# Two attentions with heads of 8: when the output of the first batch, the layer norm statistics and the store are made

## The reference

```
for l in 0..3:
    xn = layernorm(x)
    x  = x + attention_l(xn) * silu(ffn_l(xn))
```

```
Q, K, V = split(xn @ W (+ b))
w   = softmax(mask(Q K^T / sqrt(8)))
out = concat_heads(w V) @ Wo (+ bo)
```

## Time and profile before

| | us |
|---|---|
| median of 3 runs | 1969.68 |
| lowest and highest | 1960.73, 1974.17 |
| the profiled execution | 1975.89 |
| its span in the trace | 1973.2 |
| PE busy, DVE busy, ACT busy, POOL busy | 1748.1, 1442.3, 1152.1, 1038.0 |

### The profile page before, as it was taken

How to read it: one execution, slowest core, us unless ns; L and a number is a source line. 1 busy time by engine, 2 the same in 40 slices (tenths; PEclk the granted TensorE clock), 3 DMA queues, 4 the chain that set the end, 5 groups by cost and what they waited for, 6 DMA issues and landing times. The chain is left out here.

```text
span 1973.2 us, 34447 instructions
## 1 busy us (share of the span) xinstructions
PE 1748.1 (89%) x13171; PEld 1432.4 (73%) x13199; DVE 1442.3 (73%) x2911; ACT 1152.1 (58%) x2340; POOL 1038.0 (53%) x998
## 2 busy tenths in 40 slices
PE   6999999999999999899699699964798558999997
PEld 4888888888888888787567577753577445666675
DVE  6888888888888888534587677857777488777772
ACT  4677766666666667455367565542333344666665
POOL 4888999999999998920312134425257530110111
PEclk9999999999999999999899899966799878999999
DMA  3000000001000000000000000002045300000000
GB/s 89 14 1 14 1 14 1 14 1 36 1 1 1 1 1 1 28 1 1 20 17 17 0 2 1 2 22 70 22 107 134 77 14 1 1 1 1 2 2 23
DMA packets 52068, 37.44 MB, mean 19 GB/s; under 512 B 7528, under 2 KB 45832, under 8 KB 51904
## 3 DMA queue, kind: packets, MB, share of 16 engines
q1 hardware_dynamic: 45216, 30.53, 5.3%
q0 software_dynamic: 5632, 4.20, 1.5%
q10 hardware_dynamic: 1056, 0.52, 0.1%
HBM read 29.99 MB, written 5.24 MB: 18 GB/s over the span
## 5 line engine op out<-in xcount | busy, mean ns | idle before, releaser
L753 POOL TENSOR_TENSOR dtl<-dts,dth 128x512 fp32r<-128x512 f32 x256 | 346.8, 1355 | 20.5
L683 DVE TENSOR_REDUCE nm<-PS 128x1 f32<-128x1024 f32 x256 | 311.1, 1216 | 18.5 <-PE PS L203 17.7
L1884 ACT ACTIVATE ET_a<-PS 128x256 f32<-128x256 f32 (+2 forms) x512 | 221.7, 496 | 124.8 <-PE PS L1783 76.5
L751 POOL CAST dth<-dts 128x512 fp32r<-128x512 f32 x256 | 239.7, 936 | 56.2 <-ACT dts L610 55.1
L201 PE MATMUL PS<-xh,yh 128*128 128x512 f32 x512 | 225.4, 440 | 11.3 <-ACT G L603 5.7
L144 PE MATMUL PS<-C,XN 128*128 128x128 f32 x1120 | 177.6, 284 | 38.6 <-DVE XN L196 37.0
L203 PE MATMUL PS<-xh,yl 128*128 128x512 f32 x512 | 204.4, 399 | 0.0
L202 PE MATMUL PS<-xl,yh 128*128 128x512 f32 x512 | 204.2, 399 | 0.0
L603 ACT ACTIVATE XNT<-PS,nm 128x1024 f32<-128x1024 f32 x128 | 142.8, 1116 | 92.7 <-DVE nm L683 92.5
L1703 POOL TENSOR_SCALAR_AFFINE_SELECT ET_a<-ET_a 128x1024 f32<-128x1024 f32 x32 | 34.9, 1092 | 305.9 <-ACT ET_a L1884 305.9
L610 ACT ACTIVATE dts<-PS 128x512 f32<-128x512 f32 x256 | 152.8, 599 | 51.0 <-POOL dtl L753 50.9
(11 more groups left out here) (419 smaller groups left out, 4711.6 us busy)
## 6 DMA issues: line engine op xcount, KB each, us to landing
e_wg<-in_WgT SPq DMA_DIRECT2D x16, 256.0 KB
e_wu<-in_WuT SPq DMA_DIRECT2D x16, 256.0 KB
e_wd<-in_WdT SPq DMA_DIRECT2D x16, 256.0 KB
X<-in_L_attn_X SPq DMA_DIRECT2D x2, 512.0 KB, 4.5
wqn<-in_L_attn_Wq SPq DMA_DIRECT2D x8, 128.0 KB, 2.2
wkn<-in_L_attn_Wk SPq DMA_DIRECT2D x8, 128.0 KB, 2.5
wvn<-in_L_attn_Wv SPq DMA_DIRECT2D x8, 128.0 KB, 2.6
won<-in_WoT SPq DMA_DIRECT2D x8, 128.0 KB, 2.6
```

The costliest lines, as they stand in the source:

```text
L683: e.tensor_reduce(self.nm[:, half, i:i + 1], self.S[half], AX.X, MAX, negate=True).then_inc(*self.top.up((g, half)))
L751: e.tensor_copy(hi, src).then_inc(*ts.up((g, g4, "h")))
L753: e.tensor_tensor(lo, src, f(hi), SUB).then_inc(*ts.up((g, g4, "l")))
L1884: e.activation(dst, src, ACT.Exp, scale=self.SC, bias=0.0).then_inc(*self.ex.up(it))
```

## The change

1. The output of chunks 0 and 1 (whose heads are all in `XN` after head 15) is made within the drain. `fin` turns four tiles of `XN` into bank 7 and ScalarE copies them to a tile of `hm`; `finp` multiplies by `Wo` into bank 4 or 5; `sum` is VectorE's part, called `finish(c)`. Kind 3: fin and finp at (33, 1), (33, 4), (35, 1), (35, 4); sums at (34, 4), (36, 4). Kind 1: at (33, 1), (33, 7), (34, 1), (34, 7); sums at (37, 8), (37, 9).
2. Since banks 4 and 5 now hold those products, the columns of x >= 32 go round four banks instead of six.
3. In kind 1, give 29 moves from x = 39 to (36, 7), give 31 to (38, 1).
4. After the steps, PE turns chunks 2 and 3 one behind the other, then multiplies both.
5. `Gate1`: bn_stats two per step (x = 4 to 11), moments at x = 12, the 16 scalings at x = 14 to 29; GpSimd's power for it before cut_off(8) instead of (16); silus at place 13 of x = 36 and 37.
6. The bn_stats of `X` for layers 1 and 2 are taken chunk by chunk behind each chunk's sum (four each, in `Ffn0.add` and in `finish`), and `Prep` begins with the moments there. Layer 3 keeps its 16.
7. The store becomes three DMAs, of 512, 256 and 256 KB, behind the sums of chunks 1, 2 and 3.

```
@@ Ffn0.dve, add(c) @@
             e.tensor_tensor(x, x, st, ADD).then_inc(*self.on_dve.up(("add", c)))
+            q.wait_ge(self.on_dve, ("add", c))
+            for i in range(4 * c, 4 * c + 4):
+                t = e.bn_stats(k.st[:, i, :], k.X[:, i, :])
+            if c == 3:
+                t.then_inc(*self.stats.up("st"))
@@ Prep.dve @@
-        k.stats(e, k.X, self.ln, self.tag)
-        k.moments(e, q, self.ln, self.tag)
+        if not self.seen:
+            k.stats(e, k.X, self.ln, self.tag)
+        k.moments(e, q, self.ln, self.tag, self.seen)
@@ Gate1 @@
-        self.steps = [("st", i) for i in range(NT)] + [("r", 0)] + [("n", i) for i in range(NT)] + [("silu", i) for i in range(2)]
+        self.steps = [("st", i) for i in range(0, NT, 2)] + [("r", 0), ("none", 0)] + [("n", i) for i in range(NT)]
...
+    def silu(self, e, q, i):
+        gs = self.k.G[:, 8 * i:8 * i + 8, :]
+        q.wait_ge(self.ln, (8 * i + 7, 2))
+        e.activation(gs, gs, ACT.Silu, scale=1.0, bias=0.0).then_inc(*self.gated.up(i))
@@ Small.__init__ @@
+        self.fin_src = [f(x) for x in self.hm] + self.AVS
+        self.fin_bank = (4, 5, 2, 3)
...
-                elif hh == 3 and x >= 11:
+                elif hh == 3 and 11 <= x < 39:
                     self.misc[x, 1], self.misc[x, 7] = ("give", x - 10), ("give", x - 8)
+                elif x in (33, 34):
+                    self.misc[x, 1], self.misc[x, 7] = ("fin", x - 33), ("finp", x - 33)
+                elif x == 36:
+                    self.misc[x, 7] = ("give", 29)
+                elif x == 37:
+                    self.misc[x, 8], self.misc[x, 9] = ("sum", 0), ("sum", 1)
+                elif x == 38:
+                    self.misc[x, 1] = ("give", 31)
                 continue
...
+            if x in (33, 35):
+                m += [("fin", (x - 33) // 2), ("finp", (x - 33) // 2)]
+            elif x in (34, 36):
+                m += [("sum", (x - 34) // 2)]
...
             elif x == NH:
-                cs, cn = list(range(6)), 0
+                cs, cn = list(range(4)), 0
@@ Small.pe @@
+        def finish_turn(c, o, sig, event):
+            for j, n in enumerate(self.turned_of(c)):
+                t = k.tr(e, o[:, 128 * j:128 * j + 128], k.XN[:, n, :])
+            t.then_inc(*sig.up(event))
+
+        def finish_product(c):
+            o, src = self.k.bank(self.fin_bank[c]), self.fin_src[c]
+            q.wait_ge(self.fin_a, c)
+            q.wait_ge(w.in_wo, "w")
+            self.bank_done(q, self.fin_bank[c])
+            for j in range(4):
+                t = e.matmul(o[:, 128 * j:128 * j + 128], src[:, 128 * j:128 * j + 128], w.WO[:, :], start=True, stop=True)
+            t.then_inc(*self.fin_p.up(c))
...
-        for c in range(4):
-            if c >= 2:
-                q.wait_ge(self.fin_a, c - 2)
-            for j in range(4):
-                t = k.tr(e, k.bank(2 * c % 4)[:, 128 * j:128 * j + 128], k.XN[:, where[4 * c + j], :])
-            t.then_inc(*self.fin_t.up(c))
-            q.wait_ge(self.fin_a, c)
...
+        for c in (2, 3):
+            self.bank_done(q, c - 2)
+            finish_turn(c, k.bank(c - 2), self.fin_t, c)
+        for c in (2, 3):
+            finish_product(c)
@@ Small.act @@
+            elif (x, j) in self.misc and self.misc[x, j][0] == "fin":
+                u = self.misc[x, j]
+                for v in self.first_and_side[-2:]:
+                    self.hm_free(q, v)
+                q.wait_ge(self.mi_pe, u)
+                e.activation(self.fin_src[u[1]], k.bank(7), ACT.Copy).then_inc(*self.fin_a.up(u[1]))
+            if self.gate and j == 13 and x in (36, 37):
+                self.gate.silu(e, q, x - 36)
@@ Small.dve, finish(c) @@
+            q.wait_ge(self.gate.gated, c // 2)
+            e.tensor_tensor(o, sv, G, MUL).then_inc(*self.fin_d.up((c, 0)))
+            q.wait_ge(self.fin_d, (c, 0))
+            e.tensor_tensor(X, X, o, ADD).then_inc(*self.fin_d.up((c, 1)))
+            q.wait_ge(self.fin_d, (c, 1))
+            for i in range(4 * c, 4 * c + 4):
+                t = e.bn_stats(k.st[:, i, :], k.X[:, i, :])
@@ Finish.sp @@
-        e.dma_start(k.out.rearrange("b (n p) d -> p (b n) d", p=128), k.X[:, :, :]).then_inc(*self.stored.up("x"))
-        q.wait_ge(self.stored, "x")
+        for i, (c, t0, n) in enumerate(((1, 0, 8), (2, 8, 4), (3, 12, 4))):
+            q.wait_ge(s.fin_d, (c, s.fin_d.last[1]))
+            e.dma_start(k.out[t0 // 8].rearrange("(n p) d -> p n d", p=128)[:, t0 % 8:t0 % 8 + n, :],
+                        k.X[:, t0:t0 + n, :]).then_inc(*self.stored.up(i))
+        q.wait_ge(self.stored, 2)
```

More of the change, by code:

```diff
@@ L1152, with __init__ @@
 class Prep:
-    def __init__(self, k, where, tag, split):
-        self.k, self.tag, self.split = k, tag, split
+    def __init__(self, k, where, tag, split, seen=None):
+        self.k, self.tag, self.split, self.seen = k, tag, split, seen
         if split:
             self.xh, self.xl = k.sb(where, f"xh{tag}", [128, T], F32R), k.sb(where, f"xl{tag}", [128, T], F32R)
-        self.ln = k.sig("p_ln", k.norm_events(tag) + [(tag, "r")] + [("n", i) for i in range(NT)])
+        self.ln = k.sig("p_ln", k.norm_events(tag)[1 if seen else 0:] + [(tag, "r")] + [("n", i) for i in range(NT)])
         self.sq = k.sig("p_root", [tag])
@@ L1565, in __init__ @@
         first = [("project", 0, w_, ck) for w_, ck in ((1, 0), (0, 0), (1, 1), (0, 1))]
-        use = first + list(self.misc.values()) + [("give", x) for x in range(1, NH, 2) if ("give", x) not in self.misc.values()]
+        use = first + [u for u in self.misc.values() if u[0] not in ("finp", "sum")]
         self.first = first
+        assert all(("give", x) in use for x in range(1, NH, 2))
         self.prev_mi = {b: a for a, b in zip(use[4:], use[5:])}
@@ L1601, in of @@
                 mi.append(u)
-            else:
+            elif u[0] == "give":
                 mi.extend([u + (h,) for h in ("r", 0, 1)])
@@ L1626, in __init__, with side_free, bank_done, turned_of @@
         self.fin_d = k.sig("a_fin_sum", [(c, n) for c in range(4) for n in range(3 if kind == 3 else 2)])
+        self.fin_st = k.sig("a_fin_stats", ["st"])
+        self.seen = (self.fin_st, "st")
         self.ends = [(self.fin_p, 3), (self.fin_a, 3), (self.fin_d, self.fin_d.last), (self.cut, self.cut.last)]
         self.bq, self.bm = w.bq, w.bm
-    def done_of(self, u):
-        return u + (1,) if u[0] == "give" else u
+    def side_free(self, q, u):
+        a = self.prev_mi.get(u)
+        if a and a[0] == "fin":
+            q.wait_ge(self.fin_a, a[1])
+        elif a:
+            q.wait_ge(self.mi, a + (1,) if a[0] == "give" else a)
+    def bank_done(self, q, b):
+        a = self.bank_last[b]
+        q.wait_ge(self.top if a[0] == "row" else self.ex, a)
+    def turned_of(self, c):
+        where = {8 * b + self.tile_of(half, g): 8 * b + 4 * half + g for b in range(2) for half in range(2) for g in range(4)}
+        return [where[4 * c + j] for j in range(4)]
     @staticmethod
@@ L1819, in pe @@
                 side(self.misc[x, j])
-        for u in self.use:
-            if u[0] == "give" and u not in self.misc.values():
-                side(u)
-        where = {8 * b + self.tile_of(half, g): 8 * b + 4 * half + g for b in range(2) for half in range(2) for g in range(4)}
         q.wait_ge(self.mi, self.mi.last)
-        for b in range(6):
-            a = self.bank_last[b]
-            q.wait_ge(self.top if a[0] == "row" else self.ex, a)
-        for c in range(4):
-            if c >= 2:
-                q.wait_ge(self.fin_a, c - 2)
-            for j in range(4):
-                t = k.tr(e, k.bank(2 * c % 4)[:, 128 * j:128 * j + 128], k.XN[:, where[4 * c + j], :])
-            t.then_inc(*self.fin_t.up(c))
-            q.wait_ge(self.fin_a, c)
-            q.wait_ge(w.in_wo, "w")
-            if c >= 2:
-                q.wait_ge(self.fin_d, (c - 2, 0))
-            for j in range(4):
-                t = e.matmul(k.bank((2 * c + 1) % 4)[:, 128 * j:128 * j + 128], self.AVS[c % 2][:, 128 * j:128 * j + 128], w.WO[:, :],
-                             start=True, stop=True)
-            t.then_inc(*self.fin_p.up(c))
+        for c in (2, 3):
[3 more added lines that the diff above has]
+            finish_product(c)
     def act(self, e, q):
@@ L1894, in act @@
             project(u, k.bank(n))
-        late = 0
         for x, j in self.steps():
@@ L1902, in act @@
                 project(self.misc[x, j], k.bank(7))
-            if self.gate and j == 3 and x >= 4 and late < len(self.gate.steps):
-                self.gate.act_step(e, q, late)
-                late += 1
+            elif (x, j) in self.misc and self.misc[x, j][0] == "fin":
[6 more added lines that the diff above has]
+                self.gate.silu(e, q, x - 36)
             if x == 0 and j == 13:
                 clear(1, 1)
-        for c in range(4):
+        for c in (2, 3):
             q.wait_ge(self.fin_t, c)
-            if c < 2:
```

(13 more changed lines are left out.)

91 lines of the change are left out of this document (44 added, 47 removed).

## The result

Over 20 runs of each, the changed kernel takes 1961.04 us (median; 1956.76 to 1965.16) and the kernel before 1971.57 (1960.73 to 1976.12). The ratio is 0.9947 with a 95% interval of 0.9935 to 0.9960: 10.4 us less, between 7.9 and 12.8. The profiled execution took 1959.83, its span is 1957.4.

A forecast was written before the change was run, and what follows sets the result against it. No single engine bounds the kernel: PE is busy longest, layers have different limits, and the change touches only seams and drains. Gains 1.4 + 8.2 + 2.2 = 11.8 off the median 1969.68 give 1957.9, range 1949 to 1967.

The forecast's parts named there:

- Start of layer 1: Border of layers 0 and 1: eight of 16 bn_stats leave the path, 1.6 less 0.2 for waits, 1.4 gained.
- Steady part of layer 1: VectorE's Gate1 step ahead of the maxima sets group length: 1.9 lost, and 0.8 earlier possible at x = 32.
- Drain of layer 1: Layer 1, steps 33 and 34 on: turn, copy and product make the drain end 1.1 later, bounds 0 and 2.8.
- End of layer 1: Moments of layer 2 start 11.2 sooner relative to old times; first-batch sums cost nothing but fill the whole slack.
- End of layer 3: Chunks 0 and 1 are gone from the end; last sum at 1963.5 instead of 1968.12, 4.6 saved.
- Store: End of layer 3: last store 256 KB, 2.25 less waiting; rival reading of the large-transfer rule cancels it, 1960.2.
- Drain of layer 3: Steps 33 to 36: four banks and new work cost 1.85 + 0.5 + 1.85 + 0.5 = 4.7, bounds 1.0 and 7.
- A: Rival: layer 3's drain absorbs the new work and four banks, paying only 1.0; 1954.2, chance 0.18.
- B: Rival: PE's clock stays at the upper level at layer 1's end, worth about 3; 1954.9, chance 0.14.
- C: Rival, slower: PE's clock falls in layer 3's drain, costing 16; 1973.9, chance 0.04.
- D: Rival: layer 1's late sums overrun, steady part loses double, drains reach upper bounds, 2 + 2 + 4 less; 1966, chance 0.09.
- one of the forecast's signs of being wrong: Anywhere in the profile: a stretch the change does not touch moves by more than 2.

The follow-up runs named there:

- experiment 9: Kernel before with only layer 0's border bn_stats taken chunk by chunk; moments 4.67 behind the gate of chunk 2, router's reduce 18.07 behind the moments.
- experiment 6: Changed kernel with the Gate1 step of every fourth head behind both sums of the maxima; median 1955.07 us, ratio 0.9927.
- experiment 7: Changed kernel with layer 1's sum 1 behind give 31; moments of layer 2 come 14.12 behind the last mask, 1.89 earlier.
- experiment 10: Changed kernel with one 1 MB store in place of three; span ends 4.96 behind the issue, 2.35 later than with three pieces.
- experiment 1: Kernel before with four banks instead of six in layer 3's drain; steps 33 to 36 take 24.41, 2.98 more than before.
- 2: Changed kernel with both first-batch products of layer 3 in bank 5 and five banks for columns; steps 33 to 36 take 25.13, 0.76 less.
- 5: Changed kernel with layer 3's first-batch products in bank 7 and six banks for columns; steps 33 to 36 take 24.79, 1.1 less.
- experiment 3: Changed kernel with the copy of bank 7 on VectorE instead of ScalarE, both layers; odd steps 6.63 and 6.53, even ones 6.15 and 6.14.
- experiment 4: As experiment 3, with layer 3's first-batch product at place 6 instead of 4; odd steps 6.68 and 6.69, steps 33 to 36 together 25.64.
- experiment 8: On top of experiment 7, filler turns of the identity on PE; moments of layer 2 13.29 behind the last mask, layer 1's router's reduce 4.8 later.

## Why the prediction was right

The forecast was 1957.9, a ratio of 0.9940 to the median it was taken from; measured are 0.9947 and 1961.04. The base itself moved: 1969.68 over three runs, 1971.57 over twenty, which is 1.9 of the 3.1 between. The rest, 1.2, is inside the interval. The mechanism holds seam by seam, with one term, the start of layer 1, whose gain no run shows, and one, the end of layer 1, that met its number to 0.2 where the same code varies by 1.1.

- **Start of layer 1**, 1.4 gained: 1.37 to the moments, but not at the router, to which the way goes with PE's clock (experiment 9). The step said "leave the path" and stopped at the moments. From the gate of chunk 2 to the router's reduce the new code took 22.5 to 22.9 in every trace without fillers there, the old 22.4 and 27.0, so what the change is worth at the router stays open. Without this term the forecast's sum is 10.4.
- **Steady part of layer 1**, 1.9 lost and 0.8 back: the four terms that can be read match to 0.02. That the step's place is what counts is shown by experiment 6.
- **Drain of layer 1**, 1.9 from x = 32 to the last mask, measured 2.15.
- **End of layer 1**, 11.2: 11.03, and 10.0 against the 25.98 of experiment 9. "The first-batch sums cost nothing" holds against the kernel before: PE's turn of chunk 2 starts 7.56 behind the last mask in both traces. "They fill the whole slack" was too small a word. The forecast's own times had give 31 waiting 1.0 on VectorE (turn ready 1304.3, sums done 1305.3); measured are 1.97, because the clock stayed up until about 1301.2, behind the sums of head 31, and the turn was ready 4.90 behind the last mask and not 5.76. (In the trace of before the clock had fallen at 1300.1.) So 1.9 were left lying there (experiment 7).
- **End of layer 3**, 4.6: 4.90. **Store**, 2.25: 2.35, and the same by experiment 10. The rate of the old transfer, times the bytes no longer behind the last sum, was the right price, and the rival reading by the Trainium skill's rule falls.
- **Drain of layer 3**, 4.7: 4.46, and by the forecast's own measure, the loads, its parts hold too: 1.85 for an odd step was 1.68, 0.5 for an even one 0.57. The walk through step 33 had the copy done 2.2 into it, the product loaded at 3.2 and column 7 at 3.6; in the trace it is 2.17, 3.20 and 3.35. That the even steps pay less for the banks holds as well (0.64 against 0.87, experiment 1). What the experiments add: in the odd steps the number of banks makes no difference once turn and product are there (2 and 5), in the even ones all of the 0.57 is banks (5).

Of the rivals, A (the drain pays only 1.0) falls with experiment 1: the banks alone are 3.0. B (clock stays up at the end of layer 1) did not happen, and where fillers made it happen, on top of experiment 7, it was worth 0.8 and not 3. C did not happen: the drain of layer 3 ran at 1.00 with PE busy for 24.62 of 25.90. D did not either: the late sums kept the old times, and neither the steady part nor the drains reached D's bounds. By its letter one of the forecast's signs of being wrong came true, that a stretch without a change moves by more than 2: layer 0's attention moved by 5.3. The sign was set too tight, since before and experiment 1 have the same code up to layer 3 and differ there by 3.2, and by 6.0 at the gate.

How the odd steps' 1.7 divides between PE's new loads (0.59 and 0.97) and its wait for the copy (0.79) is not shown: experiment 3 left 0.61 of the wait, and experiment 4 put two waits for banks in its place. A late product with six banks would tell, and was not run. The fall of the clock at different times behind the same code is described and not explained. The 5.4 of layer 0 and the 0.8 between router and x = 4 stay open.

## What to carry to other kernels

Work that is moved into a drain whose engines have no room costs time there (here 1.7 per step that held turn and product, at both places tried), and the buffers it takes are a second price (here 0.6 per step between), which can be had back if it uses the buffer it has just emptied. Two ways of cutting a pipeline into steps give the same sum and different parts, so compare a forecast's parts with the measure they were forecast in. In a queue, put what others wait for ahead of what only has to be done: the order of two sums was worth 1.9, the place of a normalization step ahead of or behind the sum of the maxima 3.4. Add up the seams by distances between events of one trace, since the total of a profile carries the drift of every stage before.

## What the runs showed of the hardware

VectorE's operations with both inputs in SBUF that were begun while GpSimd's affine_select ran lasted up to 1.1 in place of 0.29 and ended 0.15 behind it (experiment 6; one begun 0.23 ahead of a mask kept its 0.29); reductions out of PSUM beside the same masks kept their 0.63. A tensor_scalar of 128x16 did the same there (1.07 in place of 0.17). This agrees with the Trainium skill, "SBUF — State Buffer", section "SBUF: two separate sides": the two engines share a pair of ports by an exclusive lock, not by splitting its bandwidth. In experiment 6 the mean of the last scaling step rose from 292 ns to 554 ns; whether that is what the groups miss there stays open.

The clock of PE fell at different times behind the end of its work at the border of layers 0 and 1: PE's last matmul ended at 954.04, 948.6 and 948.1 (before, after, experiment 1), and the clock fell at about 958.8, 953.0 and 949.6: 4.8, 4.4 and 1.5 later, by the granted clock of slices of 0.5 us. At the end of layer 1 it fell 1.6, 1.6 and 4.1 behind the last mask with the same code (before, experiments 1 and 9). The 40 fillers of experiment 8 started once it had fallen (0.50 from 949) and took 7.41 in place of some 4.2 at the upper level, an estimate from 0.105 each, and pushed back what stood behind them.
